# Two-layer gated cross-attention block on one core: the first norm of a half group one step ahead, new orders on VectorE and ScalarE, and the first steps' projections in other PSUM banks

## The reference

```python
x = x + tanh(g_xattn[0]) * L0_xattn(layernorm(x), ctx_1024, ctx_1024, mask)   # 16 heads of 16
x = x + tanh(g_ffn[0]) * L0_ffn(layernorm(x))      # sum over 8 experts of weight_e * (silu(x Wg_e) * (x Wu_e)) Wd_e
x = x + tanh(g_xattn[1]) * L1_xattn(layernorm(x), ctx_1024, mask)
x = x + tanh(g_ffn[1]) * L1_ffn(layernorm(x))      # top-1 expert with a capacity
```

## Time and profile before

| what | value |
|---|---|
| three runs | 884.75, 892.05, 970.44 us (median 892.05) |
| the profiled execution | 890.98 us, its span 889.1 us |
| TensorE busy | 690.4 us (78% of the span), mean granted clock 0.859 |
| VectorE busy | 542.2 us (61%) |
| GpSimd, ScalarE busy | 363.2 us (41%), 326.1 us (37%) |

### The profile page before, as it was taken

How to read it: one execution, slowest core, us unless ns; L and a number is a source line. 1 busy time by engine, 2 the same in 40 slices (tenths; PEclk the granted TensorE clock), 3 DMA queues, 4 the chain that set the end, 5 groups by cost and what they waited for, 6 DMA issues and landing times.

```text
span 889.1 us, 13079 instructions
## 1 busy us (share of the span) xinstructions
PE 690.4 (78%) x4564; PEld 571.2 (64%) x4564; DVE 542.2 (61%) x1375; ACT 326.1 (37%) x526; POOL 363.2 (41%) x251
## 2 busy tenths in 40 slices
PE   3657758869968878978889976798767874199995
PEld 3444536658757657767768865587655763189995
DVE  4663434857645675664587765767648787356662
ACT  2321314425524534533535531222133322155561
POOL 1422252446436155455337742266411213235551
PEclk8675757989979989988999997899988877589998
DMA  8400010112111021121112221123011214284530
GB/s 247 146 13 0 13 36 1 37 48 72 37 48 61 12 72 36 36 72 36 36 36 72 73 65 42 36 76 126 0 48 60 83 48 142 82 308 165 174 117 23
DMA packets 32711, 63.04 MB, mean 71 GB/s; under 512 B 3007, under 2 KB 23871, under 8 KB 32656
## 3 DMA queue, kind: packets, MB, share of 16 engines
q1 hardware_dynamic: 30592, 56.16, 18.9%
q0 software_dynamic: 2064, 6.16, 2.0%
HBM read 54.06 MB, written 8.45 MB: 70 GB/s over the span
## 4 chain that ended last, share of the span: by engine, by line
PE 62%; DVE 23%; issue 6%; ACT 3%; POOL 2%; DMA 2%; SPq 1%; DVEq 0%; ACTq 0%; POOLq 0%
PE psum L1252 41%; PE psum L1623 5%; PE psum L1355 2%; DVE arena L884 2%; PE psum L1329 2%; DVE work L833 2%; PE psum L1289 2%; PE psum L1531 1%; DVE work L864 1%; PE psum L1296 1%; DVE work L255 1%; DVE x_all L895 1%; PE psum L1323 1%; PE psum L1502 1%; PE psum L1308 1%
## 5 line engine op out<-in xcount | busy, mean ns | idle before, releaser
L1252 PE MATMUL psum<-arena 128*128 128x256 f32 (+1 forms) x2544 | 465.8, 344 | 88.4 <-DVE arena L872 37.0
L1252 PEld LDWEIGHTS psum<-arena 128*128 128x128 f32 x2544 | 399.5, 207 | 140.1 <-DVE arena L872 38.1
L1661 POOL TENSOR_TENSOR diag<-neg_ident,work 128x1024 fp32r<-128x1024 f32 x32 | 60.7, 1896 | 218.6 <-DVE work L833 207.0
L895 DVE SCALAR_TENSOR_TENSOR x_all<-psum,w_exp,x_all 128x256 f32<-128x256 f32 x128 | 56.0, 478 | 72.5 <-PE psum L1252 72.5
L879 DVE TENSOR_TENSOR work<-work,psum 128x512 f32<-128x512 f32 x64 | 43.8, 684 | 64.3 <-PE psum L1252 62.3
L559 ACT ACTIVATE arena<-work 128x512 fp32r<-128x512 f32 x64 | 40.3, 630 | 109.9 <-DVE work L879 109.9
L1672 POOL TENSOR_TENSOR arena<-work,arena 128x1024 fp32r<-128x1024 f32 x32 | 79.0, 2470 | 2.6
L884 DVE TENSOR_TENSOR arena<-work,arena 128x512 fp32r<-128x512 f32 x64 | 70.4, 1100 | 2.3 <-ACT arena L559 2.3
L552 ACT ACTIVATE work<-psum 128x512 f32<-128x512 f32 x64 | 38.2, 597 | 71.1 <-PE psum L1252 70.9
L833 DVE TENSOR_REDUCE work<-psum 128x8 f32<-128x1024 f32 x32 | 39.0, 1219 | 39.1 <-PE psum L1308 39.1
L528 ACT ACTIVATE work<-psum 128x1024 f32<-128x1024 f32 x32 | 32.8, 1025 | 75.7 <-PE psum L1329 75.5
(11 more groups left out here) (190 smaller groups left out, 938.2 us busy)
## 6 DMA issues: line engine op xcount, KB each, us to landing
work<-in_w SPq DMA_DIRECT2D x32, 768.0 KB, 4.3
work<-in_w SPq DMA_DIRECT2D x16, 1024.0 KB, 7.5
slots<-fill POOLq DMA_DIRECT2D x1, 2080.0 KB, 10.1
work<-in_ctxT SPq DMA_DIRECT2D x8, 256.0 KB, 3.9
work<-in_ctxT SPq DMA_DIRECT2D x4, 512.0 KB, 4.8
out<-x_all SPq DMA_DIRECT2D x4, 512.0 KB, 3.2
x_all<-slots SPq DMA_DIRECT2D x1, 1560.0 KB, 13.2
x_all<-in_x SPq DMA_DIRECT2D x1, 1536.0 KB, 14.3
```

Source lines behind the costliest of these rows:

```text
L895: ins = dve.scalar_tensor_tensor(x_all[:, g * GB + t, 0:D], ps[:, DN, j * D:(j + 1) * D], w_exp[g % 2][:, t, e:e + 1], x_all[:, g * GB + t ...
L1252: mm = pe.matmul(dst, left(i, k), right(j, k), start=(n == 0), stop=(n == 3 * K2 - 1))
L1661: pool.tensor_tensor(diag, neg_ident[:, :].rearrange("p (o q) -> p o q", o=1).to_broadcast([P, 8, P]), mx[u % 2].rearrange("p (h o) -> p h ...
```

## The change

- `norm0` of a half group moves from the middle of an odd step, between `maximum` and `x1_low`, to the end of the even step before it, behind `accumulate` and ahead of `routing`.
- `xn_low` and `v_add` move ahead of the step's last `h_low` and `accumulate`; on ScalarE `xn_high` moves ahead of the last `h_high`. `o_low` and the last `h_low` move ahead of an `accumulate`.
- `x1_high` moves ahead of the step's second exponential.
- In steps 0 to 3 the two projection pieces of a step leave bank TL: the first goes to GA, the second to UP, and both stand elsewhere: queries right behind the first scores, values or transposes between `o_transpose` and `o_back`, keys behind `x1_transpose`. Semaphore waits follow.
- Nothing is added or dropped in the computation; the number of instructions on each engine stays. SyncE's order is the same.

```diff
@@ -580,60 +580,70 @@
                 weights_high(n)
             act.wait_ge(s_small, 16 * 8)
             k_high(0, GA)
-            xn_high(0)
+            xn_high(0, TL)
             weights_high(3)
             act.wait_ge(s_setup.sem, 6)
             q_high(0, DN)
             ctx_high(1)
             k_high(1, GA)
-            xn_high(1)
+            xn_high(1, TL)
             act.activation(tgate[:, :], scal[:, 0:4], ACT.Tanh).then_inc(s_tanh, 1)
 
             for b in range(STEPS):
                 fa, fb = experts_of(b)
+                nxt = (b + 1) // 2 + 1
+                ahead = nxt < NH
                 if 1 <= b <= B:
                     o_copy(b - 1)
-                if b % 2 and (b + 1) // 2 + 1 < NH:
-                    ctx_high((b + 1) // 2 + 1)
+                if b % 2 and ahead:
+                    ctx_high(nxt)
                 if b < B:
                     if b == 0:
                         act.wait_ge(s_wa_lo, 4)
                     exponential(2 * b)
+                if b < GB and b % 2 == 0:
+                    q_high(nxt, GA)
                 if runs(fa):
                     silu(fa, 0)
                 if 1 <= b <= B:
                     o_high(b - 1)
+                if b < GB and b % 2:
+                    xn_high(nxt, UP)
                 if runs(fa):
                     h_high(fa, 0)
                     silu(fa, 1)
                     h_high(fa, 1)
+                if 1 <= b <= B:
+                    x1_high(b - 1)
                 if b < B:
                     exponential(2 * b + 1)
-                if 1 <= b <= B:
-                    x1_high(b - 1)
+                if b < GB and b % 2:
+                    k_high(nxt, GA)
                 if b == STEPS - 2:
                     ctx3_high(0)
                 if runs(fb):
                     silu(fb, 0)
-                if b % GB == 0 and b:
+                routed = b % GB == 0 and b and b // GB <= G
+                if routed:
                     g = b // GB - 1
-                    if g < G:
-                        act.wait_ge(lg, g + 1)
-                        if g:
-                            act.wait_ge(lgt, g)
-                        act.activation(lgT[0:E, :], ps[0:E, MX, :], ACT.Copy).then_inc(lgc, 1)
+                    act.wait_ge(lg, g + 1)
+                    if g:
+                        act.wait_ge(lgt, g)
+                    act.activation(lgT[0:E, :], ps[0:E, MX, :], ACT.Copy).then_inc(lgc, 1)
                 if runs(fb):
                     h_high(fb, 0)
-                if b % 2 and (b + 1) // 2 + 1 < NH:
-                    k_high((b + 1) // 2 + 1, TL)
-                if b % 2 == 0 and b // 2 + 1 < NH:
-                    q_high(b // 2 + 1, TL)
+                if b >= GB and ahead:
+                    if b % 2:
+                        k_high(nxt, TL)
+                    else:
+                        q_high(nxt, TL)
                 if runs(fb):
                     silu(fb, 1)
+                if b >= GB and ahead and b % 2:
+                    xn_high(nxt, TL)
+                if runs(fb):
                     h_high(fb, 1)
-                if b % 2 and (b + 1) // 2 + 1 < NH:
-                    xn_high((b + 1) // 2 + 1)
-                if b % GB == 0 and b and b // GB <= G:
+                if routed:
                     routing_exps(b // GB - 1)
 
             for s in (w4_hi, na_hi, nb_hi, k1_ok, q1_ok, e1, p1_ok, l1c, r1e):
...
@@ -1004,22 +1014,31 @@
             q_low(0, DN)
             norm0(1)
             k_low(1, GA)
-            xn_low(1)
+            xn_low(1, TL)
             maximum(0)
             small_ready()
 
             for b in range(STEPS):
                 fa, fb = experts_of(b)
+                nxt = (b + 1) // 2 + 1
+                ahead = nxt < NH
                 if b < B:
                     maximum(2 * b + 1)
+                if b < GB and b % 2 == 0:
+                    q_low(nxt, GA)
                 if 1 <= b <= B:
                     o_normalise(b - 1)
+                if b < GB:
+                    if b % 2:
+                        xn_low(nxt, UP)
+                    else:
+                        v_add(nxt, UP)
                 if runs(fa):
                     h_mult(fa, 0)
+                if 1 <= b <= B:
+                    o_low(b - 1)
                 if runs(fa - 1):
                     accumulate(fa - 1, 0)
-                if 1 <= b <= B:
-                    o_low(b - 1)
                 if runs(fa):
                     h_low(fa, 0)
                     h_mult(fa, 1)
@@ -1031,10 +1050,10 @@
                     h_low(fa, 1)
                 if b + 1 < B:
                     maximum(2 * b + 2)
-                if b % 2 and (b + 1) // 2 + 1 < NH:
-                    norm0((b + 1) // 2 + 1)
                 if 1 <= b <= B:
                     x1_low(b - 1)
+                if b < GB and b % 2:
+                    k_low(nxt, GA)
                 if b == STEPS - 2:
                     x_norm3(0)
                 if runs(fb):
@@ -1043,23 +1062,27 @@
                     accumulate(fb - 1, 0)
                 if runs(fb):
                     h_low(fb, 0)
-                if b % 2 and (b + 1) // 2 + 1 < NH:
-                    k_low((b + 1) // 2 + 1, TL)
-                if b % 2 == 0 and b // 2 + 1 < NH:
-                    q_low(b // 2 + 1, TL)
+                if b >= GB and ahead:
+                    if b % 2:
+                        k_low(nxt, TL)
+                    else:
+                        q_low(nxt, TL)
                 if runs(fb):
                     h_mult(fb, 1)
                 routed = b % GB == 0 and b and b // GB <= G
                 if routed:
                     routing_z(b // GB - 1)
+                if b >= GB and ahead:
+                    if b % 2:
+                        xn_low(nxt, TL)
+                    else:
+                        v_add(nxt, TL)
+                if runs(fb):
+                    h_low(fb, 1)
                 if runs(fb - 1):
                     accumulate(fb - 1, 1)
-                if runs(fb):
-                    h_low(fb, 1)
-                if b % 2 and (b + 1) // 2 + 1 < NH:
-                    xn_low((b + 1) // 2 + 1)
-                if b % 2 == 0 and b // 2 + 1 < NH:
-                    v_add(b // 2 + 1, TL)
+                if b % 2 == 0 and b // 2 + 2 < NH:
+                    norm0(b // 2 + 2)
                 if routed:
                     routing(b // GB - 1)
 
...
@@ -1342,10 +1365,12 @@
             def values(b):
                 h = b // 2
                 pe.wait_ge(ex, 2 * b + 2)
-                pe.wait_ge(v_ok, min(h + 2, NH) if b % 2 == 0 else h + 1)
+                pe.wait_ge(v_ok, min(h + 2, NH) if b % 2 == 0 and b >= GB else h + 1)
                 if b:
                     pe.wait_ge(x1_lo, b)
-                if b % 2 and h + 2 < NH:
+                else:
+                    pe.wait_ge(xt_lo, 2)
+                if b % 2 and b >= GB and h + 2 < NH:
                     pe.wait_ge(xt_lo, h + 3)
                 for gp in range(2):
                     for j in range(2):
@@ -1418,26 +1443,48 @@
...
+            def first_piece(b, bank):
+                h = (b + 1) // 2 + 1
+                if b % 2:
+                    k_project(h, bank)
+                else:
+                    q_project(h, bank)
+
+            def second_piece(b, bank):
+                h = (b + 1) // 2 + 1
+                if b % 2:
+                    xn_transpose(h, bank)
+                else:
+                    v_project(h, bank)
+
             for b in range(STEPS):
                 fa, fb = experts_of(b)
+                nxt = (b + 1) // 2 + 1
                 if 1 <= b <= B:
                     values(b - 1)
                 if b < B:
                     scores(2 * b)
+                if b < GB and b % 2 == 0:
+                    pe.wait_ge(k_lo, b + 4)
+                    first_piece(b, GA)
                 if 1 <= b <= B:
                     o_transpose(b - 1)
+                if b < GB:
+                    pe.wait_ge(v_ok, (b + 1) // 2 + 1)
+                    pe.wait_ge(xt_lo, b // 2 + 2)
+                    second_piece(b, UP)
                 if runs(fa):
                     gate_up(fa, 0)
                 if 1 <= b <= B:
@@ -1454,34 +1501,33 @@
                     scores(2 * b + 1)
                 if 1 <= b <= B:
                     x1_transpose(b - 1)
+                if b < GB and b % 2:
+                    pe.wait_ge(q_lo, b + 3)
+                    first_piece(b, GA)
+                if b == GB:
+                    pe.wait_ge(k_lo, 2 * nxt + 2)
+                    pe.wait_ge(xt_lo, nxt + 1)
                 if runs(fb):
                     gate_up(fb, 0)
                 routed = b % GB == 0 and b and b // GB <= G
                 if routed:
                     pe.wait_ge(x1_lo, b)
                     logits0(b // GB - 1)
-                nxt = (b + 1) // 2 + 1
-                if nxt < NH:
-                    if b:
```

(14 more changed lines are left out.)

18 lines of the change are left out of this document (9 added, 9 removed).

## The result

The changed kernel takes 816.75 us (median of 4 runs, 814.23 to 823.72), the kernel before 892.43 (4 runs, median). The ratio of the means is 0.919, with a 95% interval of 0.910 to 0.928; one disturbed run of the kernel before, of 970.44 us, is left out of it. The profiled execution took 816.5 us (span 814.7) where that of before took 891.0: 74.5 us less, where the prediction had summed 53.5.

A forecast was written before the change was run, and what follows sets the result against it. It took TensorE's pipeline waits, mid odd step and at step ends, and the slower clock behind them as the bound: 891.0 - 54.1 (waits and clock) + 20.6 (new order's cost) - 20 (steps 0 to 3) = 837.5 us, range 828 to 849.

The forecast's parts named there:

- Parts 1 and 3: Waits for `x1_low` in steps 5, 7, 9, 11: -22.6 us; step-end waits -16.8 and clock behind them -7.5.
- The middle wait: TensorE's wait for `x1_low` in front of a projection, steps 5, 7, 9, 11; goes altogether, -22.6 us.
- the ends: Step-end waits: -9.0 us at odd ends, -7.8 at even ends; clock in steps 8, 9, 10, 12, 13: -7.5.
- Part 2: Slow clock behind the `x1_low` waits of steps 5, 7, 9, 11 goes: 1.8 us each, -7.2 us.
- I take the middle: Steps 1 to 3: -18.5 us, between 49.5 us at full clock and 65.8 at half clock.
- part 5: Steps 0 to 3 get shorter with the new order: -20 us (-12 to -28), of which step 0 -1.4.
- part 3: Step ends: waits in front of `values` shrink, -16.8 us; five steps no longer begin at half clock, -7.5.
- Part 4: New order's cost, +20.6 us: steps 7 and 11 +3.0, 5 +6.0, 9 +8.2, 13 +2.4, ScalarE's table load +1.0.
- The 1.8 us of clock: Steps 5 and 9: clock drops behind the longer wait in front of `o_back`, +1.8 us in each.
- Better than summed: Rival, chance 0.09: shorter steps 1 to 4 run at full clock and step 5's clock holds, 824 us.
- no wait changed its name in the middle: Rival, chance 0.05: odd steps' keys or `h_mult` are late where `x1_low` was; 867 us.
- ScalarE's switch: Rival, chance 0.03: later `silu` of the second expert lengthens steps 5 to 16 by 1.5 us each; 918 us.

The follow-up runs named there:

- the fill: Matmuls that nothing reads put into TensorE's waits of steps 1 to 3: in the changed kernel 812.76 us, in the kernel before 881.84 us.
- `c_norm`: Changed kernel with the norm of steps 4 and 8 done in steps 5 and 9 behind `x1_low`, and `o_copy` between the routing exponentials: 816.28 us.

## Why the prediction was right in sign and short in size

**Parts 1 and 3 were right.** The middle wait went altogether (22.6 us, and 22.6 came back in the same four steps with the norm); the ends were summed at 24.3 and are worth 26.6 when taken back. Part 2 took its 1.8 us from step 7 alone: in the kernel before the 36 matmuls of steps 5, 7, 9 and 11 took 7.50, 8.33, 8.50 and 8.40, against 6.7 that is 5.9 and not 7.2. The norm costs 3.9 us at its new place, and steps 7 and 11 show 0.33 us in front of `o_back` and 0.85 in front of `x1_transpose`, forecast 1.5 together. Step 7 took 28.01 (28 to 29).

**The step that failed is the clock, at "I take the middle" in part 5.** It was taken over from the kernel before, as if it were a property of the place, when it follows from the waits that the change removes. Steps 1 to 3 took 48.1 us where the middle was 57.5: that is 9.3 of the 21 us. The clock was given 8.0 of the 57.5, and cost 1.2: with the fill these steps ran at 1.00 and took 46.9. The other 2.6 are the chain, which the prediction had summed at 49.5 for full clock. Six other executions with the same steps 1 to 3 took 48.4 to 50.5 for them, and a second one with the fill 45.4, so the clock costs 1 to 5 us there and in none of them the 8.0. The fill in the kernel before shows the direction of cause: with waits filled and no other work changed, steps 2 and 3 of the same chain ran at 1.00 instead of 0.50 and 0.70. Not all of the 27.8 us is clock: the banks shorten the chain by 14.2 at nearly the same clock.

**Step 4 got no term** (4.1 us). It was 31.68 us because it began at half clock; part 3 counted such starts for steps 8, 9, 10, 12 and 13 and left this one out. With the fill it began at full clock and took 26.35.

**Part 4 priced steps 5 and 9 too high** (2.2 and 2.8 us). The delay of `o_back` was right (13.8 and 14.3 us after the start, forecast 13.5 and 14.2). The 1.8 us of clock added behind it did not come in the profiled execution: `o_copy`, which no step of the prediction had followed, was held up behind the routing exponentials and split the wait, and the loss of clock fell into the stretch between. For `c_norm`, where the wait is in one piece, the loss is there: 8.01 against 6.57.

Three more kernels have VectorE's order of step 5, and their traces show what of it was luck (us):

| kernel | twelve of `gate_up` | wait for `o_normalise` | `o_back` after the start | the 42 behind it | step 5 |
|---|---|---|---|---|---|
| changed | 5.13 | 1.27 | 13.82 | 6.57 | 34.68 |
| early projections back in TL | 4.59 | 2.16 | 13.84 | 8.14 | 35.20 |
| `x1_high` late | 3.02 | 3.74 | 13.83 | 8.14 | 35.41 |
| fill in the changed kernel | 4.59 | 2.18 | 13.85 | 8.10 | 35.21 |

A loss of clock ahead of the second wait is free: `o_back` comes at 13.8 in all four. But behind it the clock fell too, in three of the four. That cost 0.5 to 0.7 us and not 1.8, since the wait of 0.87 in front of `x1_transpose` is then gone. In step 9 the 42 took 6.57 or 6.58 in all four.

**Small terms.** Step 13 became 3.0 us longer, where the sum left 1.2: its wait for `o_normalise`, 3.60, is in one piece, the 42 matmuls behind it took 7.84, and no clock was counted there. `x1_high`'s table load shows as two waits of 0.54, forecast 0.3 in each of three steps, which is nearly the same.

**The rivals.** "Better than summed" (824, at 0.09) named the mechanism, a full clock in the short steps and in step 5, and priced it at 13 us, where the whole miss was 21. Of what spoke against the forecast, nothing came: no wait changed its name in the middle, and ScalarE's switch decided nothing. Two signs of being right didn't come either: the wait of 7 us in front of `o_back` in steps 5 and 9 came as two, of 4.3 and 5.0 us together, and step 4 started at 93.8 and not near 103.

**What stays open.** The parts taken back singly leave 5 of the 74.4 us; with single steps varying by 1.6 us between executions this is not to be assigned. Nothing is known of why step 1 begins anywhere between 42.5 and 46.4 us in the kernels whose step 0 is that of the changed one (in the two executions of one program at 42.49 and 45.67); so what step 0 gained is not shown.

Open too is which clock follows a wait. Steps 5 and 6 of the kernel before with the fill, where nothing was added, are 2.5 us longer than without it. Behind a wait for `o_normalise` of 2.53 us its 42 matmuls took 8.17, where they had taken 6.58 behind one of 2.51; and `values` of step 6 took 1.89, where it had taken 1.08, behind the same 2.26 us. So the length of the wait alone doesn't decide it. The loss behind `c_norm`'s wait is an observation of this kind, and not a price that can be relied on.
